# Two blocks of attention and experts on one core: gate products moved to GpSimd, the second attention reordered, zero products added

## The chip, the cores and the metric

The kernel runs on one core of one Trainium2 chip. The metric is the device time of one execution in microseconds (us); lower is better. TensorE (PE) multiplies matrices into PSUM, VectorE (DVE) and ScalarE (ACT) read and write SBUF and PSUM, GpSimd (POOL) works here on SBUF alone, SyncE issues most DMAs. Each engine runs its own instructions in program order and waits on semaphores for the others.

## The reference

`x` is (8 sequences, 128 tokens, 128 channels), float32. Four residual steps follow one another, each on a layer norm of `x`:

```python
x = x + tanh(g_xattn[0]) * xattn0(layernorm(x), ctx, ctx)   # 16 heads of 64, causal mask
x = x + tanh(g_ffn[0])   * ffn0(layernorm(x))               # 8 experts of 256 + 4 zero experts, best 2 of 12
x = x + tanh(g_xattn[1]) * xattn1(layernorm(x), ctx, ctx)   # 16 heads of 8, biases, no mask
x = x + tanh(g_ffn[1])   * ffn1(layernorm(x))               # 8 routed experts of 64, best 2 of 8, + 2 shared

# ffn1
logits = xf @ router_w + router_b
gates  = softmax(logits of the best 2, 0 elsewhere)
expert = lambda xf, w1, w3, w2: silu(xf @ w1) * (xf @ w3) @ w2
out    = sum_e gates[:, e] * expert_e(xf) + sum of the two shared experts
```

The change touches the third step (the second attention) and the fourth (the second expert step).

## The kernel before

The program is written per engine, as five lists of instructions with semaphores between them; the order on each engine is the order of the calls in its block. Three PSUM tensors of two banks (`SP`, `TP`, `OC`) are handed round by hand. The fourth, `MB`, is a ring of two banks: `ring_order()` lists every use of it in the order in which TensorE takes them, use k lies in bank k % 2, and `take(name)` makes TensorE wait until use k - 2 has been read. A new order on TensorE therefore needs a new ring order, and each use waits for the reader of the one two before it.

Second attention, sequence by sequence b = 0 to 7. `scores1(b, j)` (L1238, 32-row products, j = 0, 1 for two of the four head groups) fills an area; `max1` on DVE (L882) takes its maxima into `NM`; `maxima1(b)` on TensorE (L1258) transposes them into the ring; `shift1(b)` on DVE (L890) adds them to the queries, so that `turned1(b, j)` (L1250) gives shifted scores the other way round; `exp1(b, j)` on ACT (L571) takes their exponentials; `values_of(b)` (L1267) and `sums_of(b)` (L1274) multiply by the values and sum up; `copy_outputs(b)` on ACT (L580) and `normalise1(b)` on DVE (L895 to L906) and POOL (L414) finish them. In the loop TensorE's order for b = 3 to 6 is `values_of(b-2)`, `maxima1(b)`, `scores1(b+1, 0)`, `scores1(b+1, 1)`, `sums_of(b-2)`, `turned1(b, 0)`, `turned1(b, 1)`. DVE's is `shift1(b)`, `max1(b+1, 0)`, `max1(b+1, 1)`, `normalise1(b-2)`. The queries of sequences 4 to 7 are laid out by four products `spread_queries(i)` (L1206, L1207) and four copies `place_queries(i)` on ACT (L563); before, all four copies stand behind `exp1(1, 1)`. `output1(h, w)` (L1287) is the output projection of two sequences, `residual` on DVE (L767) adds it, statistics, `rstd_of` on POOL (L379, L380) and `normed` on DVE (L694) make the layer norm, `xn_transposes(n, h)` (L1047) turns it, `xnT_hi_copy` on ACT (L494) and `xnT_lo_copy` on DVE (L701, L702) split it in two parts; `three` (L1026 to L1028) multiplies with both.

Second expert step, ten turns n = 0 to 9 (two halves of the tokens, five pairs of experts; n = 0 and 5 are the shared pair and have no gates). `hidden1(n)` on TensorE makes the two hidden halves (six 512-column products), `silu_1(n)` on ACT (L587) takes silu of the first, `hidden1(n)` on DVE multiplies by the second (L914) and, for a routed pair, by the gates (L921), which `spread_gates(n)` (L1335) has spread over the rows in a ring bank; `expert1(n)` (L1315) is the second matrix. The gates come from `logits` (L1146), `route_best` and `route_gates` on DVE (L783 to L823) with `best_difference` on POOL (L418), `gates_turn` (L1326), `gates_hi` on ACT (L596) and `gates_lo` on DVE (L925).

`keep_clock(dst, times)` (L1033) issues products of zeros, 128 x 256 in bfloat16, whose results nobody reads: 20 at the start, 12 in `fill_wait(0)`, 10 in `gates_turn(0)`.

Of the kernel before, what the change touches and what calls it, by code (L numbers as in the profile page):

```python
# [12 lines left out]
ALU = mybir.AluOpType  # L13
# [30 lines left out]
def ring_order():  # L44
# [13 lines left out]
    uses += [("a", 2, 0), ("a", 2, 1), ("w", 0), ("t", 2, 1), ("m", 1), ("q1", 1), ("o", 0), ("m", 2)]  # L58
    uses += [("p", i) for i in range(4)]
    for b in range(3, B):  # L60
        uses += [("m", 7), ("y1", 0, 0), ("y1", 0, 1), ("o", 5)] if b == 7 else [("o", b - 2), ("m", b)]
    uses += [("o", B - 2), ("t", 3, 0), ("o", B - 1), ("l", 1, 0)]
    uses += [("y1", 1, 0), ("y1", 1, 1), ("g", 0), ("b", 1), ("t", 3, 1)]
    for n in range(2, N1):
        if pair1(n) < C1 - 1:
            uses.append(("b", n))
        uses += {2: [("l", 1, 1)], 4: [("g", 1)]}.get(n, [])
# [15 lines left out]
def build(nc, x, ctxT, mask, g_x, g_f, w0, wo0, bo0, gw0, gb0, f0w1, f0w2,  # L83
          wqk1, bqk1, wv1, bv1, wo1, bo1, gw1, gb1, f1w13, f1w2,
          ident, causal, k_rows, zeros, pairs, rev0, rev1, out):
    with ExitStack() as ctx:
# [35 lines left out]
        rstd = sb("rstd", [P, B])  # L122
        euler = sb("euler", [P, HB])
# [13 lines left out]
        S_sb = sb("S_sb", [P, 2, H4, P])  # L137
        PT = sb("PT", [P, 2, H4, P])
# [103 lines left out]
        h1_full, silu1, up1, y1_full = (sem(n) for n in ("h1_full", "silu1", "up1", "y1_full"))  # L242
        fin, stored = sem("fin"), sem("stored")
# [15 lines left out]
        def ring_read(kind, a, b=0):  # L259
# [6 lines left out]
                    "b": (up1, 2 * a + 2)}[kind]  # L266
# [102 lines left out]
        def _(pool):  # L369
# [49 lines left out]

            g.memset(warm_sb[:], 0.0).then_inc(warm_set, 1)  # L420
# [27 lines left out]
            hooks = {0: [lambda: add_bias(2, 1)], 2: [lambda: split_f1(0), lambda: split_f1(1)],  # L448
                     3: [lambda: split_f1(2), lambda: split_f1(3)], 7: [lambda: rstd_of(3, 0)]}
# [6 lines left out]
            best_difference(1, 0)  # L456
            rstd_of(3, 1)
            best_difference(1, 1)

        @block.scalar  # L460
        def _(act):
# [196 lines left out]
            hooks = {2: [lambda: split_f1(0), lambda: split_f1(1)], 3: [lambda: split_f1(2), lambda: split_f1(3)]}  # L658
# [11 lines left out]
            hooks = {1: [lambda: gates_hi(0)], 2: [lambda: xnT_hi_copy(3, 1)], 5: [lambda: gates_hi(1)]}  # L670
# [6 lines left out]
        def _(dve):  # L677
# [19 lines left out]
            def xnT_lo_copy(n, h):  # L697
                name = ("t", n, h)
                dve.wait_ge(hi_, nth(n, h))
                if n % 2:  # L700
                    v.tensor_copy(xnT[:], ring(name)).then_inc(flat_, 1)  # L701
                ins = v.tensor_tensor(xnT_lo[:, half(h)], ring(name), xnT_hi[:, half(h)].bitcast(F32), ALU.subtract)  # L702
# [205 lines left out]
            def hidden1(n):  # L908
                h, c = n // C1, pair1(n)
                dve.wait_ge(silu1, n + 1)  # L910
# [4 lines left out]
                if c == C1 - 1:  # L915
# [63 lines left out]
            max1(2, 1)  # L979
            mid = {7: [lambda: residual(1, 0, 0), lambda: residual(1, 0, 1),  # L980
                                                       lambda: stats_after(3, 0)]}
            late = {7: [lambda: normed(3, 0)]}
            for b in range(2, B):
# [6 lines left out]
                normalise1(b - 2)  # L990
# [3 lines left out]
            xnT_lo_copy(3, 0)  # L994
            normalise1(B - 1)
            route_best(1, 0)
            residual(1, 1, 0)
            residual(1, 1, 1)
# [499 lines left out]
```

## Time and profile before

| | us |
|---|---|
| median of 3 runs | 271.07 |
| lowest, highest | 268.44, 273.26 |
| the profiled execution | 270.25 |
| its span, first to last instruction | 268.5 |
| mean granted TensorE clock of the span | 0.985 |

The profiled execution lies 0.8 us under the median; 1.75 us of it lie outside the span. The three runs spread over 4.8 us, 1.8% of the median. The granted clock is a share of full speed: 1.00 is TensorE's 2.4 GHz and 0.50 its 1.2 GHz.

### The profile page before, as it was taken

What the parts mean: (1) busy time and instruction counts of PE and PEld (TensorE: products, weight loads), DVE (VectorE), ACT (ScalarE), POOL (GpSimd) and SP (SyncE); (2) the same over time, 40 slices, a digit from 0 to 9 for tenths busy, and PEclk for the clock granted to TensorE, in tenths of its full rate; (3) what the DMA queues carried; (4) which work ended last, traced back from release to release, by engine and by line L of the source; (5) the groups of instructions that cost most, each with busy time, mean ns of one, the idle gap of its engine ahead of it and who ended that gap; (6) DMA issues with size and microseconds to landing.
All of it is one profiled execution on the core that took longest, in us unless ns stands there. A gap on an engine that the chain in (4) does not pass through costs nothing.

```text
span 268.5 us, 7171 instructions
## 1 busy us (share of the span) xinstructions
PE 246.7 (92%) x2914; PEld 208.4 (78%) x2914; DVE 187.4 (70%) x487; ACT 116.2 (43%) x199; POOL 73.0 (27%) x92
## 2 busy tenths in 40 slices
PE   8879999899999999989999999998899988879993
PEld 3557778788998888768999998987577877657882
DVE  1637788967374998897256695466897994879753
ACT  2565455544441555414134445423378643421310
POOL 3355393445433633340010013000306013111000
PEclk9999999999999999999999999999799988999999
DMA  7619500040000000087680000620000000000011
GB/s 194 197 55 306 147 1 4 2 120 4 0 2 2 1 2 2 2 273 275 240 281 1 2 0 0 182 94 4 0 2 2 2 2 2 2 2 2 0 39 39
DMA packets 13233, 16.74 MB, mean 62 GB/s; under 512 B 2065, under 2 KB 10641, under 8 KB 13073
## 3 DMA queue, kind: packets, MB, share of 16 engines
q1 hardware_dynamic: 13056, 16.03, 19.0%
q8 instruction: 23, 0.38, 0.6%
q10 hardware_dynamic: 144, 0.26, 0.4%
q14 instruction: 10, 0.07, 0.1%
HBM read 12.62 MB, written 3.67 MB: 61 GB/s over the span
## 4 chain that ended last, share of the span: by engine, by line
PE 72%; DVE 14%; issue 4%; ACT 4%; POOL 2%; DMA 2%; DVEq 0%; SPq 0%
PE OC L1176 11%; PE MB L1136 5%; PE MB L1026 5%; PE SP L1097 5%; PE OC L1119 5%; PE TP L1106 5%; PE MB L1028 4%; PE MB L1027 4%; PE TP L1315 3%; PE MB L1267 2%; PE OC L1125 2%; PE SP L1026 2%; PE SP L1028 2%; PE SP L1027 2%; PE MB L1274 2%
## 5 line engine op out<-in xcount | busy, mean ns | idle before, releaser
L409 POOL TENSOR_TENSOR S_sb<-S_sb,nmax 128x512 f32<-128x512 f32 x32 | 33.2, 1041 | 38.8 <-DVE nmax L742 38.8
L839 DVE SCALAR_TENSOR_TENSOR x_sb<-OC,gate,x_sb 128x128 f32<-128x128 f32 x64 | 18.0, 345 | 22.5 <-PE OC L1176 22.5
L1176 PEld LDWEIGHTS OC<-f_w,hid 128*128 128x128 f32 x256 | 30.9, 192 | 1.4
L733 DVE TENSOR_TENSOR S_sb<-SP,maskb 128x512 f32<-128x512 f32 x32 | 21.9, 686 | 14.0 <-PE SP L1097 13.8
L1176 PE MATMUL OC<-f_w,hid 128*128 128x128 f32 x256 | 31.4, 276 | 0.0
L742 DVE TENSOR_REDUCE nmax<-S_sb 128x4 f32<-128x512 f32 x32 | 22.0, 686 | 1.1
L525 ACT ACTIVATE PT<-TP 128x512 f32<-128x512 f32 x32 | 19.0, 594 | 7.2 <-PE TP L1106 7.1
L1106 PE MATMUL TP<-id_sb,S_sb 128*128 128x128 f32 x128 | 19.5, 275 | 1.9 <-POOL S_sb L409 1.8
L1119 PE MATMUL OC<-PT,arena_f 128*32 128x128 f32 x512 | 17.7, 275 | 2.8 <-issue 2.1
L509 ACT ACTIVATE arena_f<-MB 128x512 f32<-128x512 f32 x16 | 9.6, 599 | 23.7 <-PE MB L1028 23.2
L501 ACT ACTIVATE arena_f<-MB 128x512 f32<-128x512 f32 x16 | 9.6, 599 | 23.2 <-PE MB L1028 22.4
L379 POOL TENSOR_SCALAR var_eps<-mv 128x4 f32<-128x4 f32 x8 | 2.0, 247 | 62.5 <-DVE mv L687 62.5
L1106 PEld LDWEIGHTS TP<-id_sb,S_sb 128*128 128x128 f32 x128 | 14.9, 141 | 5.0 <-POOL S_sb L409 3.4
L1097 PE MATMUL SP<-arena_f 64*128 64x128 f32 x256 | 18.6, 285 | 0.0
L1097 PEld LDWEIGHTS SP<-arena_f 64*128 64x128 f32 x256 | 15.5, 187 | 2.6 <-issue 1.8
L1119 PEld LDWEIGHTS OC<-PT,arena_f 128*32 128x32 f32 x512 | 13.3, 109 | 5.5 <-issue 4.4
L558 ACT ACTIVATE hid<-SP 128x512 f32<-128x512 f32 x16 | 9.5, 598 | 17.4 <-PE SP L1028 16.8
L558 ACT ACTIVATE hid<-TP 128x512 f32<-128x512 f32 x16 | 9.6, 599 | 14.8 <-PE TP L1028 13.8
L1136 PE MATMUL MB<-wo_sb,oT 128*128 128x128 f32 x128 | 15.0, 276 | 0.0
L1136 PEld LDWEIGHTS MB<-wo_sb,oT 128*128 128x128 f32 x128 | 14.6, 192 | 0.2 <-issue 0.2
L1315 PEld LDWEIGHTS TP<-f_w,hid 128*128 128x128 f32 x80 | 9.9, 191 | 5.5 <-DVE hid L921 3.3
L1315 PE MATMUL TP<-f_w,hid 128*128 128x128 f32 x80 | 11.1, 281 | 3.3 <-DVE hid L921 2.3
(202 smaller groups left out, 587.9 us busy)
## 6 DMA issues: line engine op xcount, KB each, us to landing
k_dram<-f_r SPq DMA_DIRECT2D x4, 512.0 KB, 8.7
arena_f<-in_zeros SPq DMA_DIRECT2D x1, 2048.0 KB, 8.6
arena_r<-k_dram SPq DMA_DIRECT2D x1, 2048.0 KB, 8.1
w_raw<-in_w SPq DMA_DIRECT2D x4, 384.0 KB, 4.0
ew_raw<-in_f0w SPq DMA_DIRECT2D x1, 1024.0 KB, 6.4
f_w<-in_f0w SPq DMA_DIRECT2D x1, 1024.0 KB, 10.3
arena_r<-q_dram SPq DMA_DIRECT2D x2, 512.0 KB, 4.1
ew_raw<-in_f1w SPq DMA_DIRECT2D x1, 640.0 KB, 9.8
```

The costliest lines, as they stand in the source:

```text
L409: g.tensor_tensor(S_sb[:, b], S_sb[:, b], nmax[:, b].unsqueeze(2).to_broadcast([P, H4, P]), ALU.add).then_inc(shifted, 1)
L525: sc.activation(PT[:, b], TP[:, b, :].rearrange("p (h q) -> p h q", h=H4), ACT.Exp).then_inc(expd, 1)
L558: sc.activation(hid[:, n % 2, c, :], bank[:, c, :], ACT.Silu).then_inc(hid_done, 1)
L733: v.tensor_tensor(S_sb[:, b].rearrange("p (r a) k -> p r a k", r=2), SP[:, :, 2 * P * b:2 * P * (b + 1)].rearrange("p r (a k) -> p r a k", ...
L742: v.tensor_reduce(nmax[:, b], S_sb[:, b], X, ALU.max, negate=True).then_inc(maxed, 1)
L1026: mm(out_, w[0], m[0], start=True, stop=False)
L1097: ins = mm(SP[:, r, P * (2 * b + p):P * (2 * b + p + 1)], qT[rows, s % 2, p, o], kT[rows, s % 2, p, o], start=True, stop=True)
L1106: ins = nc.tensor.transpose(TP[:, b, P * i:P * (i + 1)], S_sb[:, b, i, :], id_sb[:])
L1119: mm(OC[32 * hd:32 * (hd + 1), 0, P * (2 * a + b):P * (2 * a + b + 1)], v0[:, s % 2, 2 * w + b, DH0 * hd + 32 * a:DH0 * hd + 32 * (a + 1)] ...
L1136: ins = mm(bank[:, batch(b)], oT[:, k, batch(2 * w + b)], wo_sb[:, k, :], start=(k == 0), stop=(k == 7))
L1176: ins = mm(OC[:, n % 2, batch(t)], hid[:, n % 2, c, batch(t)], f0_w2[:, e, c, :], start=(c == 0), stop=(c == 1))
L1315: ins = mm(TP[:, h, batch(t)], hid[:, n % 2, 1, batch(t)], f1_w2[:, c, :], start=(first and t == 0), stop=last, skip_group_check=True)
```

## The change

What it does, stage by stage:

- The expert step: for n = 1 to 4 the gates are copied from the ring to SBUF by ACT (`gates_rows`, into the old score tile, renamed `gate_rows`), POOL multiplies silu by them (`gate_silu`), and DVE does one product instead of two. Turns 6 to 9 stay as they were. `silu_1` waits for the first hidden half alone. `output1(1, 1)`, `gates_turn(0)`, `expert1(0)`, the transposes and the logits of the second half, and the last `spread_gates` stand elsewhere in TensorE's order; residuals and statistics stand behind the first `hidden1` on DVE; `route_best(1, 0)` stands ahead of the last `normalise1`, `sums_of(7)` behind the logits.
- The flat copy of the fourth norm's transposes moves from DVE to ACT; DVE's split waits for it.
- Two one-column activations into a `spare` tile, one with Exp behind the last silu of the first expert step, one with Silu between the last outputs of the attention.
- The second attention: `spread_queries` and `place_queries` come earlier, among `turned1(1, *)` and `exp1(1, *)`; `maxima1(3)` comes ahead of `turned1(2, *)`; the splits of the expert weights (`split_f1`, ACT and POOL) come two sequences later; `normalise1(0)` comes earlier on DVE.
- Zero products: 8 ahead of `turned1(0, 0)`, 16 instead of 12 in `fill_wait`, 3, 8, 4, 4, 4, 4 ahead of the maxima of b = 2 to 7, 6 ahead of `output1(0, 1)`, 4 instead of 10 in `gates_turn(0)`. The four each at b = 4, 5 and 6 stand ahead of the fifth to the seventh maxima.

```diff
@@ ring_order
-    uses += [..., ("m", 1), ("q1", 1), ("o", 0), ("m", 2)]
-    uses += [("p", i) for i in range(4)]
+    uses += [..., ("m", 1), ("q1", 1), ("o", 0)]
+    uses += [("p", 0), ("p", 1), ("m", 2), ("p", 2), ("p", 3)]
...
+                 [("m", 3), ("o", 1)] if b == 3 else [("o", b - 2), ("m", b)])
-    uses += [("y1", 1, 0), ("y1", 1, 1), ("g", 0), ("b", 1), ("t", 3, 1)]
+    uses += [("y1", 1, 0), ("g", 0), ("y1", 1, 1), ("b", 1)]
...
+        uses += {2: [("t", 3, 1), ("l", 1, 1)], 4: [("g", 1)]}.get(n, [])
@@ gpsimd
+            def gate_silu(n):
+                pool.wait_ge(rows_full, n)
+                pool.wait_ge(silu1, n + 1)
+                g.tensor_tensor(hid[:, n % 2, 0, :], hid[:, n % 2, 0, :], gate_rows[:, n % 2, :], ALU.mult
+                                ).then_inc(gated_silu, 1)
...
             best_difference(1, 0)
+            gate_silu(1)
             rstd_of(3, 1)
+            gate_silu(2)
+            gate_silu(3)
             best_difference(1, 1)
+            gate_silu(4)
@@ scalar
+            def xnT_flat_copy(h):
+                name = ("t", 3, h)
+                wait_full(act, name)
+                act.wait_ge(logit_in, nth(1, 0) if h else nth(0, 1))
+                sc.activation(xnT[:], ring(name), ACT.Copy).then_inc(flat_, 1)
...
-                act.wait_ge(h1_full, n + 1)
+                act.wait_ge(h1_full, 2 * n + 1)
...
+            def gates_rows(n):
+                wait_full(act, ("b", n))
+                if n > 2:
+                    act.wait_ge(gated_silu, n - 2)
+                sc.activation(gate_rows[:, n % 2, :], ring(("b", n)), ACT.Copy).then_inc(rows_full, 1)
...
+            sc.activation(spare[:], tanh_g[:, 0:1], ACT.Exp)
             exp1(0, 0)
             exp1(0, 1)
             xnT_hi_copy(2, 1)
             queries1(1)
             copy_outputs(0)
+            place_queries(0)
+            place_queries(1)
             exp1(1, 0)
+            place_queries(2)
+            place_queries(3)
             exp1(1, 1)
-            for i in range(4):
-                place_queries(i)
-            hooks = {2: [... split_f1(0), split_f1(1)], 3: [... split_f1(2), split_f1(3)]}
+            hooks = {4: [... split_f1(0), split_f1(1)], 5: [... split_f1(2), split_f1(3)]}
...
             copy_outputs(B - 3)
+            sc.activation(spare[:], tanh_g[:, 0:1], ACT.Silu)
             copy_outputs(B - 2)
             xnT_hi_copy(3, 0)
+            xnT_flat_copy(0)
             copy_outputs(B - 1)
+            hooks = {1: [gates_hi(0), gates_rows(1)],
+                     2: [gates_rows(2), xnT_hi_copy(3, 1), xnT_flat_copy(1)],
+                     3: [gates_rows(3)], 4: [gates_rows(4)], 5: [gates_hi(1)]}
@@ vector
             def hidden1(n):
+                dve.wait_ge(h1_full, 2 * n + 2)
+                by_pool = 0 < n < C1
+                if by_pool:
+                    dve.wait_ge(gated_silu, n)
+                else:
+                    dve.wait_ge(silu1, n + 1)
...
-            route_best(1, 0)
-            residual(1, 1, 0)
-            residual(1, 1, 1)
-            hooks = {0: [route_gates(1, 0), stats_after(3, 1), gates_lo(0), normed(3, 1)], 1: [xnT_lo_copy(3, 1)],
-                     2: [route_best(1, 1)], ...
+            route_gates(1, 0)
+            hooks = {0: [residual(1, 1, 0), gates_lo(0), residual(1, 1, 1), stats_after(3, 1)],
+                     1: [normed(3, 1)], 2: [xnT_lo_copy(3, 1), route_best(1, 1)],
...
@@ tensor
+                if b == j == 0:
+                    keep_clock(bank[:, 0, 0:256], 8)
...
+            ZEROS = {2: 3, 3: 8, 4: 4, 5: 4, 6: 4, 7: 4}
+
             def maxima1(b):
                 name = ("m", b)
                 bank = take(name)
+                if b in ZEROS:
+                    keep_clock(bank[:, 256:512], ZEROS[b])
                 pe.wait_ge(maxed1, 2 * (b + 1))
...
-                    keep_clock(bank[:, 256:512], 10)
+                    keep_clock(bank[:, 256:512], 4)
...
             outputs1(0)
+            spread_queries(0)
+            spread_queries(1)
             turned1(1, 0)
             turned1(1, 1)
             maxima1(2)
             scores1(3, 0)
             scores1(3, 1)
-            spread_queries(0) ... spread_queries(3)
+            spread_queries(2)
+            spread_queries(3)
+            maxima1(3)
+            scores1(4, 0)
             turned1(2, 0)
             turned1(2, 1)
+            values_of(1)
+            scores1(4, 1)
+            sums_of(1)
+            turned1(3, 0)
+            turned1(3, 1)
+            for b in range(4, B):
...
                     output1(0, 0)
+                    keep_clock(area_for("t", b, 0)[:, 0, 0:256], 6)
                     output1(0, 1)
...
-            outputs1(B - 1)
+            values_of(B - 1)
             logits(1, 0)
+            sums_of(B - 1)
             hidden1(0)
+            hidden1(1)
             output1(1, 0)
+            gates_turn(0)
+            expert1(0)
             output1(1, 1)
-            hidden1(1)
-            expert1(0)
-            gates_turn(0)
-            hidden1(2)
             spread_gates(1)
-            xn_transposes(3, 1)
+            hidden1(2)
             expert1(1)
             for n in range(2, N1):
-                if pair1(n) < C1 - 1:
+                if pair1(n) < C1 - 1 and n < N1 - 1:
                     spread_gates(n)
                 if n == 2:
-                    logits(1, 1)
+                    xn_transposes(3, 1)
                 if n + 1 < N1:
                     hidden1(n + 1)
+                if n == 2:
+                    logits(1, 1)
+                if n == N1 - 2:
+                    spread_gates(N1 - 1)
                 if n == 4:
                     gates_turn(1)
                 expert1(n)
```

## Rows read from the trace of the kernel before

**Rows 1.** Windows: PE, PEld, DVE, ACT, POOL busy, granted clock, DMA share, GB/s.
```profile
185.40:188.80 3.40, 1.56 (x27) 1.26 (x27) 3.21 (x13) 2.56 (x3) 0.67 (x2) 1.00 0.02 5
188.80:192.20 3.40, 3.40 (x19) 2.45 (x18) 2.55 (x6) 0.82 (x2) 1.87 (x2) 0.51 0.00 0
192.20:219.60 27.40, 24.98 (x538) 19.99 (x537) 24.04 (x37) 18.30 (x27) 5.63 (x9) 1.00 0.01 2
219.60:222.90 3.30, 3.30 (x59) 2.92 (x61) 1.74 (x9) 1.94 (x2) 1.12 (x2) 0.50 0.02 5
222.90:264.00 41.10, 35.78 (x348) 29.79 (x338) 30.41 (x92) 10.68 (x18) 4.37 (x7) 1.00 0.03 8
```

**Rows 2.** Timeline, start of the second attention: start us, us, instructions, idle before them.
```profile
186.23 1.28 ACT L571 ACT_TABLE_LOAD   x1 [4.58 <-PE MB L1250]
...
187.52 1.02 ACT L571 ACTIVATE oT<-MB 128x1024 f32<-128x1024 f32 x1
...
188.60 2.55 PE L1033 MATMUL MB<-warm_sb 128*128 128x256 bf16 x12 [1.24 <-ACT oT L571]
189.44 1.14 DVE L694 SCALAR_TENSOR_TENSOR xn<-x_sb,mv,rstd 128x128 f32<-128x128 f32 x4 [0.36 <-POOL rstd L380]
```

**Rows 3.** Timeline, the zero products of gates_turn(0).
```profile
236.04 1.26 PE L1033 MATMUL MB<-warm_sb 128*128 128x256 bf16 x10
```

**Rows 4.** Timeline: the first place_queries, and the maxima of b = 4, 5 and 7.
```profile
198.90 1.08 ACT L563 ACTIVATE arena_r<-MB 128x512 fp32r<-128x512 f32 x2
...
206.52 0.33 PE L1258 MATMUL MB<-id_sb,NM 128*128 128x128 f32 x1
...
210.37 0.33 PE L1258 MATMUL MB<-id_sb,NM 128*128 128x128 f32 x1
...
217.68 0.30 PE L1258 MATMUL MB<-id_sb,NM 128*128 128x128 f32 x1 [0.56 <-DVE NM L882]
```

**Rows 5.** Timeline, end of the second attention and start of the routing.
```profile
220.76 1.94 PE L1267 MATMUL MB<-arena_f 128*32 128x128 f32 x32
...
225.13 1.30 DVE L694 SCALAR_TENSOR_TENSOR xn<-x_sb,mv,rstd 128x128 f32<-128x128 f32 x4
...
227.13 1.08 PE L1267 MATMUL MB<-oT,arena_f 128*32 128x128 f32 x32
...
229.22 1.06 PE L1146 MATMUL MB<-gw_sb,xnT 128*128 128x8 f32 x8
...
229.57 0.31 DVE L895 STREAM_TRANSPOSE sumT<-o_sb 128x128 f32<-128x128 f32 x1 [0.41 <-ACT o_sb L580]
...
230.76 0.18 DVE L794 TENSOR_TENSOR logit<-MB,gb_sb 128x32 f32<-128x32 f32 x1
...
233.53 0.88 DVE L767 SCALAR_TENSOR_TENSOR x_sb<-MB,tanh_g,x_sb 128x256 f32<-128x256 f32 x2
```

**Rows 6.** Timeline, route_gates' first and last, expert1 of n = 0, 1, 4, 9.
```profile
234.91 0.17 DVE L808 TENSOR_SCALAR rs<-rs 128x4 f32<-128x4 f32 x1
235.05 0.97 PEld L1315 LDWEIGHTS TP<-f_w,hid 128*128 128x128 f32 x8 [1.44 <-DVE hid L914]
...
235.85 0.22 DVE L823 TENSOR_TENSOR gate<-rt 128x64 f32<-128x64 f32 x1
...
241.82 1.16 PE L1315 MATMUL TP<-f_w,hid 128*128 128x128 f32 x8 [0.79 <-DVE hid L921]
...
251.66 1.06 PE L1315 MATMUL TP<-f_w,hid 128*128 128x128 f32 x8
...
264.00 1.16 PE L1315 MATMUL TP<-f_w,hid 128*128 128x128 f32 x8 [1.07 <-DVE hid L921]
```

**Rows 7.** Groups of instructions by form: busy, mean ns of one, idle before.
```profile
L409 POOL TENSOR_TENSOR S_sb<-S_sb,nmax 128x512 f32<-128x512 f32 x32 | 33.2, 1041 | 38.8 <-DVE nmax L742 38.8
...
L392 POOL TENSOR_TENSOR f_lo<-ew_raw,f_hi 128x512 fp32r<-128x512 f32 x4 | 5.1, 1272 | 7.4 <-ACT f_hi L476 7.4
...
L921 DVE TENSOR_TENSOR hid<-hid,MB 128x512 f32<-128x512 f32 x8 | 5.5, 688 | 0.8
```

More of the change, by code:

```diff
@@ L122, in build @@
         rstd = sb("rstd", [P, B])
+        spare = sb("spare", [P, 1])
         euler = sb("euler", [P, HB])
@@ L265, in ring_read @@
                     "p": (placed, a + 1), "a": ((maxed1, 1), (maxed1, 2), (expd1, 1))[a if kind == "a" else 0],
-                    "b": (up1, 2 * a + 2)}[kind]
+                    "b": (rows_full, a) if a < C1 else (up1, 2 * a + 2)}[kind]
         def area_read(kind, b, j):
@@ L447, in _ @@
             rstd_of(2, 1)
-            hooks = {0: [lambda: add_bias(2, 1)], 2: [lambda: split_f1(0), lambda: split_f1(1)],
-                     3: [lambda: split_f1(2), lambda: split_f1(3)], 7: [lambda: rstd_of(3, 0)]}
+            hooks = {0: [lambda: add_bias(2, 1)], 4: [lambda: split_f1(0), lambda: split_f1(1)],
+                     5: [lambda: split_f1(2), lambda: split_f1(3)], 7: [lambda: rstd_of(3, 0)]}
             for b in range(B):
@@ L699, in xnT_lo_copy @@
                 dve.wait_ge(hi_, nth(n, h))
-                if n % 2:
+                if n == 1:
                     v.tensor_copy(xnT[:], ring(name)).then_inc(flat_, 1)
+                elif n == 3:
+                    dve.wait_ge(flat_, nth(1, h))
                 ins = v.tensor_tensor(xnT_lo[:, half(h)], ring(name), xnT_hi[:, half(h)].bitcast(F32), ALU.subtract)
@@ L979, in _ @@
             max1(2, 1)
+            normalise1(0)
             mid = {7: [lambda: residual(1, 0, 0), lambda: residual(1, 0, 1),
@@ L989, in _ @@
                     hook()
-                normalise1(b - 2)
+                if b > 2:
+                    normalise1(b - 2)
                 for hook in late.get(b, ()):
@@ L994, in _ @@
             xnT_lo_copy(3, 0)
+            route_best(1, 0)
             normalise1(B - 1)
-            route_best(1, 0)
-            residual(1, 1, 0)
-            residual(1, 1, 1)
-            hooks = {0: [lambda: route_gates(1, 0), lambda: stats_after(3, 1), lambda: gates_lo(0), lambda: normed(3, 1)], 1: [lambda: xnT_lo_copy(3, 1)],
-                     2: [lambda: route_best(1, 1)], 3: [lambda: route_gates(1, 1)], 4: [lambda: gates_lo(1)],
+            route_gates(1, 0)
+            hooks = {0: [lambda: residual(1, 1, 0), lambda: gates_lo(0), lambda: residual(1, 1, 1), lambda: stats_after(3, 1)],
+                     1: [lambda: normed(3, 1)], 2: [lambda: xnT_lo_copy(3, 1), lambda: route_best(1, 1)],
+                     3: [lambda: route_gates(1, 1)], 4: [lambda: gates_lo(1)],
                      5: [lambda: finish(0, 0), lambda: finish(0, 1)]}
@@ L1037, in fill_wait @@
                 name = ("w", b)
-                done(name, keep_clock(take(name)[:, 0:256], 12))
+                done(name, keep_clock(take(name)[:, 0:256], 16))
             def xn_transposes(n, h):
@@ L1303, in hidden1 @@
                     o = slice(2 * P * c + P * k, 2 * P * c + P * (k + 1))
-                    ins = three((OC, SP)[n % 2][:, k, :], (f1_hi[:, o], f1_lo[:, o]), (xnT_hi[:, half(h)], xnT_lo[:, half(h)]))
-                ins.then_inc(h1_full, 1)
+                    three((OC, SP)[n % 2][:, k, :], (f1_hi[:, o], f1_lo[:, o]), (xnT_hi[:, half(h)], xnT_lo[:, half(h)])
+                          ).then_inc(h1_full, 1)
             def expert1(n):
@@ L1403, in _ @@
             scores1(3, 1)
-            spread_queries(0)
-            spread_queries(1)
+            spread_queries(2)
+            spread_queries(3)
+            maxima1(3)
+            scores1(4, 0)
             turned1(2, 0)
-            spread_queries(2)
             turned1(2, 1)
-            spread_queries(3)
-            for b in range(3, B):
+            values_of(1)
[4 more added lines that the diff above has]
+            for b in range(4, B):
                 if b == B - 1:
```

18 lines of the change are left out of this document (10 added, 8 removed).

## Prediction

> **What bounds the kernel now.** I read the granted clock by windows first, then the timeline of the last 80 us, then the groups by form. Up to 185 us nothing changes, so the question is the last third. There the clock is at half speed twice, for about 3.4 us each [rows 1]. Ahead of the first dip PE was busy 1.56 of 3.40 us [rows 1]: it waits for the exponentials of sequence 0, which wait for an activation table load of 1.28 us [rows 2]. The second dip falls where the last maxima and the output projection alternate with DVE. Between the dips the clock is full for 27.4 us with PE busy 24.98 and DVE 24.04 [rows 1]: the attention loop holds both engines at once. A turn of it takes 210.37 - 206.52 = 3.85 us [rows 4]. In the expert step the clock is full throughout [rows 1]; its first turns follow a chain through DVE (PE waits for L921 at n = 1), the last ones are PE-bound [rows 6].
>
> I followed the new orders by hand, with durations from these rows, and give the result at milestones, as shift against before.
>
> **First maxima to the fifth, +1.0.** The Exp load goes to where ACT idled before (4.58 us, [rows 2]), so 1.28 us leave the path. But the 8 zero products ahead of `turned1(0, 0)` stand on it: one costs 1.26/10, some 0.11 us started back to back at full clock [rows 3], so 0.86 us, and score products that ran beside each other are parted, 0.4 more. The first exponential starts where it did. `fill_wait` gets 16 products: 1.7 us at full clock against 2.55 for 12 at half [rows 2]. If the clock holds, the transposes start as soon as `normed` is done at 190.58, 0.7 us earlier in the end. That gain is spent at once. `spread_queries` 0 and 1 now stand ahead of `turned1(1, *)`, and their two copies (0.54 each, [rows 4]) ahead of `exp1(1, 0)`; the next two stand ahead of `exp1(1, 1)`, which moves from 197.9 to about 200.9 and holds `turned1(2, *)`. I find the third maxima at +0.4, the fourth earlier (they no longer wait for `turned1(2, *)`), and the fifth at 207.5 against 206.52, four zero products among it: +1.0. A table load hidden that costs nothing needs ACT idle; it is.
>
> The Trainium skill (ScalarE: Activation LUTs, What ACT_TABLE_LOAD costs) adds a drain of about 1.38 us to each load; here the exponential starts at 187.52, right behind the load that began at 186.23 [rows 2], so 1.28 is taken off and not 2.66. By the page this stage would come out 1.4 us better, and the whole at 270.6.
>
> **Fifth to seventh maxima, +0.9.** The loop's ring goes: maxima, shift on DVE, `max1(b+1, 0)` on DVE, `turned1(b, 1)`, `values_of`, next maxima. Four zero products between `values_of` and the maxima lengthen it by 0.43, since PE does not wait for DVE there: the maxima come 3.3 us after the last ones' start, PE is there at 3.85. Two more sets, at b = 5 and 6: 0.86. The clock was full there already [rows 1], so nothing is bought. The set at b = 7 falls into the 0.56 us in which PE waits for L882 [rows 4], the 6 at `output1(0, 1)` into a wait of about the same length: nothing. If that cover were gone they would cost 0.43 and 0.64.
>
> **To `normed(3, 0)`, -1.4.** If the second dip goes, 32 products of `values_of` cost 1.08 us and not 1.94 [rows 5], and with the turned scores and the sums some 1.5 us leave the path through `copy_outputs(5)` and `normalise1(5)`, on which `normed` at 225.13 [rows 5] waited in DVE's order. So `normed(3, 0)` starts at about 225.6: +0.4 in all. The Silu load stands between two copies with 1.4 us between them; it moves nothing.
>
> **To `expert1(0)`, +1.0.** ACT now makes the flat copy (0.6 us) ahead of DVE's split, in place of DVE's own 0.69: even. `sums_of(7)` waits behind the logits, whose bank needs that split (ring use k - 2), so it moves from 228.0 to about 230.4, and `hidden1(0)` from 230.1 to 231.4. DVE does `route_best` first (230.76 to 233.5, 2.8 us [rows 5]), which covers this; then `normalise1(7)`, 229.57 to 230.76 before, 1.2 us [rows 5]; then `route_gates`, 234.91 to 236.07 [rows 6]. From logits that end at 230.4: 230.5 + 2.85 + 1.2 + 1.2 = 235.75, gates 0.3 us earlier. POOL's power of 1 us hides behind `normalise1(7)`. But the first product of `hidden1(0)` now stands behind the gates on DVE: 235.75 + 0.7, so `expert1(0)` starts at 236.45 against 235.05 [rows 6]: +1.4 in all.
>
> **To `expert1(1)`, -2.1.** Behind it DVE does one residual (0.45), `gates_lo`, the other residual and statistics; PE spreads the gates at about 237.95. ACT copy 0.6, POOL product, one DVE product 0.69 [rows 7]. POOL's product is not in the trace: two full 128 x 512 inputs, so I take L392's 1.27, the nearest; L409's 1.04, with one input a repeated column, is the low end; with DVE working beside it I allow 1.5 as the high end (an estimate, 1.27 and a fifth). `expert1(1)` starts at 238.4 + 0.65 + 1.35 + 0.75 = 241.15 against 241.82 [rows 6]: -0.7 in all. The `normed(3, 1)` that stood ahead of it on DVE comes behind, and POOL's `rstd_of(3, 1)` waits for the first `gate_silu`.
>
> **To `expert1(4)`, +3.2.** Here the change is a longer chain: `spread_gates(n)` is issued behind `expert1(n-1)`, and then spread, ACT copy, POOL product, DVE product follow in series: 0.95 (expert products) + 0.25 + 0.2 + 0.65 + 1.3 + 0.75 = 4.15 with handovers. Before, the ring bank was read by DVE directly, and expert 1 to 4 took 251.66 - 241.82 = 9.84 us [rows 6], 3.3 a turn. After: 241.15, 245.8 (waits for the late `normed(3, 1)` and the logits too), 249.95, 254.15. ACT and PE have time to spare there; `hidden1(n+1)` of 1.4 us fits in the chain. So DVE loses one product of 0.69 a turn and gains nothing: +2.5 in all.
>
> **To the end, -0.7.** Turns 6 to 8 are PE-bound before and after (2.54 us each). The last `expert1` waited for silu and two products [rows 6]; silu now starts at the first half, 0.6 earlier, and the last spread costs PE nothing on that chain: 265.8 against 264.00, +1.8.
>
> The sum: +1.0 + 0.9 - 1.4 + 1.0 - 2.1 + 3.2 - 0.7 = +1.8 (with rounding). Against the profiled execution's own 270.25 that gives 272.0, span 270.3. The median shown is 0.8 above the profiled time; I leave it out, because what sets runs apart may be dips of this kind, and the change removes two. Bounds: POOL at 1.04 or 1.5 moves four links by 0.23 each: -0.9, +0.9; hand-overs in the followed orders, 1 us either way.
>
> The Trainium skill (GPSIMD Engine Reference, Performance versus the Vector engine) measures a two-input float32 product of 2048 columns at 4497 ns; a quarter is 1.12 us, an estimate. By it the sum would be 0.6 lower. Its Engine selection section gives elementwise products to VectorE, which speaks against this move; the chain above agrees.
>
> **Rivals.**
> (a) *The gates chain is no loss.* If DVE's own order (`route_best`, `route_gates`, normalisations) really set turns 2 to 4, the freed products pay: DVE is busy 30.41 of the last 41.10 us [rows 1]. Then those turns stay at 3.3 and 2.5 of the 3.2 fall away; with POOL at 1.04 another 0.9: 268.6. If further low-clock stretches that this one execution does not show are usual before (273.26 is 3 us above it), a median after could lie another 2 to 4 lower: 265 to 266. Against it: the hand-over count above.
> (b) *The zeros do not hold the clock.* They don't do what they are for: in one or both old places it still falls. Each costs what it cost: 0.7 and 1.5, and 16 zero products at half clock take 3.4 us and not 1.7, 0.9 more. 272.0 + 2 to 3 = 274.5.
> (c) *New waits bring new dips.* PE now waits 0.9 us for `normed(3, 0)` and 1.1 us more for the split at 228.4 to 229.5 with little work between, about as much idle time as ahead of the first dip (1.84 of 3.4 us, [rows 1]); and 1.4 us a turn for the gates at n = 1, 3 and 4. A dip at half clock over 3.4 us of PE-bound work costs up to 1.7 us; over the chained turns about 1. It is slower by over 2% only if four or five fall, or with POOL at 1.5: two dips and 0.9 give 276, three 277.5. For it: such waits did bring dips. Against it: the waits at n = 0 and 1 before were about 1 us and the clock stayed full [rows 1].
>
> **Chances.** Forecast as summed, dips gone, 0.45. (a) 0.25, of it 0.1 under 2%. (b) 0.12. (c) 0.18, half of it beyond 2%. 2% is 5.4 us, about what a measurement of this kernel, whose three runs spread over 4.8 us, tells from no change. Faster 0.12, within 2% 0.78, slower 0.10. The range: from (a)'s upper part, 267.0, to (c) with two dips, 276.0.
>
> **What would show it.** Right: clock 1.00 from 186 to 225; maxima 4.28 us apart at b = 4 to 6; ACT's Exp load at about 181.7; `normed(3, 0)` near 225.6; expert1 of n = 1 to 4 over 4 us apart, each waiting for the DVE product behind POOL; POOL products near 1.27 us. Wrong: turns of 3.3 us, a half-clock window between 225 and 255, or maxima still 3.85 apart.

## The result and the profile after

| | before | after |
|---|---|---|
| median of 4 runs each | 272.16 us | 280.06 us |
| lowest, highest | 268.44, 273.47 | 279.14, 280.99 |
| after / before, 95% interval | | 1.038 (1.027 to 1.049) |
| profiled execution | 270.25 | 279.14 |
| its span and mean granted clock | 268.5, 0.985 | 277.4, 0.973 |

The change makes the kernel 3.8% slower. The ratios leave out executions in the slower of two states: here 280.06 stands against before's 268.44 and 271.07, for e1 to e4 before is three executions at 268.0, and for the later kernels it is executions of 268.0 to 272.0, so kernels of different groups are compared by their spans. The four spans after are 277.2 to 279.2 at clocks of 0.963 to 0.973. Before ran 70 times more beside the runs below. One of these took 1310.75 us at full clock and is left out; the other 69 have a mean span of 270.4 and clocks of 0.959 to 1.000. In the eight with the clock at 0.999 or more the span is 266.2 to 266.6; I take 266.4. I call such a span, with next to no time at half clock, a clean one.

Windows of the kernel after (columns as in [rows 1]):

```profile
188.80:192.20 3.40, 2.55 (x20) 1.90 (x20) 3.04 (x6) 1.67 (x3) 2.06 (x3) 1.00 0.00 0
...
197.30:200.70 3.40, 3.04 (x41) 2.24 (x38) 2.62 (x6) 2.14 (x4) 0.46 (x1) 1.00 0.03 5
200.70:214.30 13.60, 13.28 (x166) 10.17 (x168) 5.21 (x8) 6.65 (x10) 1.43 (x3) 0.50 0.00 1
214.30:272.90 58.60, 50.78 (x678) 41.99 (x674) 41.58 (x115) 23.77 (x38) 14.41 (x18) 1.00 0.02 6
```

Both half-clock stretches of [rows 1] are gone, as forecast. A third, longer one has come: 200.7 to 214.3. In it PE is busy 13.28 of 13.60 us, DVE only 5.21: the attention waits for TensorE at 1.2 GHz. The timeline shows what TensorE did as it fell:

```profile
198.54 0.66 PE L1282 MATMUL TP<-arena_r 32*128 32x128 f32 x8
...
199.16 0.66 PE L1282 MATMUL OC<-arena_r 32*128 32x128 f32 x8
...
199.66 0.44 PE L1250 MATMUL MB<-q_hi,ctxT_lo 32*128 32x512 f32 x2
...
199.94 0.39 PE L1251 MATMUL MB<-q_lo,ctxT_lo 32*128 32x512 f32 x2
200.37 1.08 ACT L583 ACTIVATE arena_r<-MB 128x512 fp32r<-128x512 f32 x2 [1.26 <-PE MB L1251]
...
201.03 1.89 PE L1077 MATMUL MB<-warm_sb 128*128 128x256 bf16 x8 [0.69 <-ACT arena_r L583]
```

They are score products and `spread_queries`, each on 32 rows of the array, and then TensorE waits 0.69 us for `place_queries`. The eight zero products of the fourth maxima come at 201.03, after the fall, and take 1.89 us where [rows 3] has ten in 1.26; the clock stayed low behind them.

The milestones by which the prediction went, as start us:

| | before | after | shift | forecast |
|---|---|---|---|---|
| first exponential | 187.52 | 188.38 | +0.9 | 0 |
| fourth maxima, b = 3 | 201.98 | 202.71 | +0.7 | earlier |
| fifth maxima, b = 4 | 206.52 | 213.56 | +7.0 | +1.0 |
| seventh maxima, b = 6 | 214.21 | 222.39 | +8.2 | +1.9 |
| `normed(3, 0)` | 225.13 | 231.69 | +6.6 | +0.4 |
| `expert1(0)` | 235.05 | 242.62 | +7.6 | +1.4 |
| `expert1(1)` | 241.82 | 247.48 | +5.7 | -0.7 |
| `expert1(4)` | 251.66 | 261.17 | +9.5 | +2.5 |
| `expert1(9)` | 264.00 | 272.89 | +8.9 | +1.8 |

Of the 0.9 at the first exponential, 0.7 were there at the first maxima already (183.30 against 182.63). So nearly the whole miss lies between the first maxima and the fifth, and 6.3 us of it between the fourth and the fifth.

### The profile page after: what moved, and what is told of

Same layout as the page of the kernel before. It is cut to its first block, busy times and chain, and to the rows that moved or that the text cites. A ratio compares the mean times of both kernels' runs of the same rounds, so it can differ in the third digit from the quotient of the medians.

```text
span 277.4 us, 7260 instructions
## 1 busy us (share of the span) xinstructions
PE 255.4 (92%) x2953; PEld 214.0 (77%) x2953; DVE 185.1 (67%) x481; ACT 119.8 (43%) x207; POOL 78.2 (28%) x96
## 4 chain that ended last, share of the span: by engine, by line
PE 75%; DVE 9%; issue 4%; POOL 4%; ACT 4%; DMA 2%; POOLq 0%; DVEq 0%; SPq 0%; ACTq 0%
PE OC L1220 10%; PE MB L1180 5%; PE MB L1070 5%; PE SP L1141 5%; PE OC L1163 5%; PE TP L1150 4%; PE MB L1071 4%; PE MB L1072 4%; PE MB L1077 3%; PE TP L1365 3%; PE MB L1317 2%; PE MB L1324 2%; PE SP L1070 2%; PE OC L1169 2%; DMA w_raw<-in_w 2%
## 6 DMA issues: line engine op xcount, KB each, us to landing
f_w<-in_f0w SPq DMA_DIRECT2D x1, 1024.0 KB, 10.2
```

## The experiments

Three stages are taken apart: the zero products, the order around `spread_queries` (below, the spread order), and the expert step. The first four start from the kernel after; the `f` kernels build the change up from a version without these three; `g` and `h` follow up. In the code cuts some lines are shortened, several calls stand on one line, and lines that follow from those shown are left out. Clocks and spans are those of single executions. A mean clock does not say where the half clock fell: before's 17 executions at 0.967 span 271.5 to 274.2. So a comparison at a like clock is rough.

**e1_no_loop_zeros.** Leaves out the four zeros each at b = 4, 5, 6.

```diff
-            ZEROS = {2: 3, 3: 8, 4: 4, 5: 4, 6: 4, 7: 4}
+            ZEROS = {2: 3, 3: 8, 7: 4}
```

> The changed kernel without the four zero products each at b = 4, 5 and 6. Theory 1 (the loss is the 13.5 us at half clock that begin at 200.7 us, ahead of these products): the dip stays, and these products cost 0.43 us each at full clock and 0.9 at half (one set): 278 to 279. Theory 2 (they help the clock back up after the dip): without them the dip lasts longer, 281 or more. Theory 3 (they are themselves the loss): below 276.

Median 277.56 (276.59 to 278.50), 1.035 (1.029 to 1.042) of before, between the ranges of theories 1 and 3. At a clock of 0.973 the span is 276.1 and 275.4, against 277.4 after: 1.3 and 2.0 for three sets, of which the one at b = 4 lies in the half-clock stretch. Timeline of the kernel after, the zeros and the maxima of b = 5, then those of b = 6:

```profile
217.71 0.61 PE L1077 MATMUL MB<-warm_sb 128*128 128x256 bf16 x4
...
218.15 0.27 PE L1308 MATMUL MB<-id_sb,NM 128*128 128x128 f32 x1
...
222.39 0.27 PE L1308 MATMUL MB<-id_sb,NM 128*128 128x128 f32 x1
```

The same maxima of e1:

```profile
217.25 0.33 PE L1308 MATMUL MB<-id_sb,NM 128*128 128x128 f32 x1
...
221.10 0.33 PE L1308 MATMUL MB<-id_sb,NM 128*128 128x128 f32 x1
```

A turn takes 4.24 with four zeros and 3.85 without, which is that of before [rows 4]: 0.39 a set at full clock, where 0.43 was summed. The long half-clock stretch is there in e1 too, so these zeros neither cause nor cure it.

**e2_old_spread.** The order of `spread_queries`, `place_queries` and the fourth maxima as before, in the ring, on ACT and on PE.

```diff
-    uses += [("p", 0), ("p", 1), ("m", 2), ("p", 2), ("p", 3)]
+    uses += [..., ("m", 2)]
+    uses += [("p", i) for i in range(4)]
-                 [("m", 3), ("o", 1)] if b == 3 else [("o", b - 2), ("m", b)])
+        uses += (... if b == 7 else [("o", b - 2), ("m", b)])
...
-            place_queries(0), place_queries(1), exp1(1, 0), place_queries(2), place_queries(3), exp1(1, 1)
+            exp1(1, 0), exp1(1, 1), place_queries(0) ... place_queries(3)
...
-            spread_queries(0) ... spread_queries(3), maxima1(3), turned1(2, 0), turned1(2, 1)
+            spread_queries(0), spread_queries(1), turned1(2, 0), spread_queries(2), turned1(2, 1), spread_queries(3)
+            for b in range(3, B):
```

> The changed kernel with spread_queries, place_queries and the fourth maxima back in the order of before; all zero products stay. Theory 1 (the new order with its thin work and its wait for the copies lets the clock fall at 200.7): the dip is gone, 5 to 6 us back, 273 to 275. Rival (the new expert step makes the loss): no change within 1 us, 279 to 281.

Median 275.15 (274.22 to 275.39), 1.025 (1.020 to 1.031). Clocks 0.981 to 0.991, spans 272.4 to 273.3: the long stretch is gone and 5 us with it. In its profile a short one, 3.4 us, stands in the expert step, between 250.5 and 254.5.

**e3_old_experts.** The expert step as before, everything else as after: gates multiplied on DVE, old order on all engines.

```diff
-                by_pool = 0 < n < C1
+                by_pool = False
...
```

> The changed kernel with the whole expert step of before (gates on DVE, its order on every engine). Theory 1: the dip at 200.7 stays, and only the chain through POOL goes, worth the +1.8 that stood at the end of my sum against +0.4 at the start of the fourth norm, plus 0.9 for one DVE instruction held while POOL worked: 277 to 279. Rival (the expert step makes the loss): 272 to 273.

Median 276.10 (273.23 to 279.07), 1.026 (1.010 to 1.043); spans 271.4 to 277.2 at clocks 0.985 to 0.960. The half-clock stretch is still there (200.9 to 211.2 in its profile). So it is a matter of the attention.

**e4_zeros_at_spread.** Eight zeros more, between the two pairs of `spread_queries`.

```diff
+                if i == 2:
+                    keep_clock(bank[:, 0:256], 8)
```

> The changed kernel with 8 more zero products, into the ring bank of the third spread_queries ahead of it, 0.86 us at full clock on the path. Theory 1 (too little work in the stretch before 200.7): the dip goes, 5 to 6 us back less 0.9: 274 to 276. Rival (zero products do not hold the clock there, or the dip has another cause): 280 to 281.

Median 279.35 (274.31 to 283.06): two executions with clocks of 0.999 and 0.988 and spans of 272.5 and 273.9, two with 0.957 and spans of 281.1 and 281.2. It holds half the time. The execution at 0.999 is the only one that shows the whole change at a full clock: 272.5 less 0.86 for these eight zeros makes 271.6 for the kernel after, an estimate from one execution, against 266.4 before. So 5.2 of the slowdown is work and order.

The profiled execution, the one at 0.988, keeps the clock in the attention; two short half-clock stretches, 3.4 us each, stand in its expert step, between 244.0 and 248.0 and between 254.5 and 258.5. So it shows the new spread order at full clock:

```profile
197.30:200.70 3.40, 3.40 (x41) 2.69 (x40) 2.68 (x4) 1.47 (x2) 0.45 (x1) 1.00 0.02 5
200.70:214.30 13.60, 12.87 (x295) 10.31 (x295) 9.18 (x15) 10.02 (x15) 3.19 (x5) 1.00 0.01 2
...
208.81 0.27 PE L1310 MATMUL MB<-id_sb,NM 128*128 128x128 f32 x1
```

The last line is its fifth maxima, 4.75 us ahead of those of the kernel after, with eight zeros more.

**f0_base.** From the kernel after, without the loop zeros, with the old spread order and the old expert step. What is left of the change are the early table loads, `split_f1` later, `normalise1(0)` earlier, and the other zeros.

```diff
-            ZEROS = {2: 3, 3: 8, 4: 4, 5: 4, 6: 4, 7: 4}
+            ZEROS = {2: 3, 3: 8, 7: 4}
...    (and the edits of e2 and of e3)
```

> The changed kernel with the old expert step, the old order of spread_queries, place_queries and the fourth maxima, and without the zero products at b = 4, 5 and 6: what stays are the early table loads, the later weight splits, the earlier normalise1(0) and the zero products at b = 0, 2, 3, 7 and in fill_wait. Theory (these zeros hold the clock in the two old places, and nothing else of the change is needed for that): clock 0.995 or more in every execution, 266 to 268. Rival (the clock falls all the same): 270 to 273 with executions far apart.

Median 270.11 of 10 runs (268.24 to 273.11), 0.997 (0.992 to 1.002). Mean clock 0.992, mean span 268.4; clean spans 266.4 to 266.9, up to 0.5 above before's 266.4. This part of the change costs next to nothing and steadies the clock: three of ten executions at 0.999 or more, eight of 69 before. Against what I had expected, it does not hold it in every execution: in its profile the clock is still at half for 3.4 us between 188.5 and 192.5, the first of the two old places.

**f1_base_new_experts, f2_base_new_spread, f3_base_pool_gates.** One part added to f0 each: the whole new expert step; the new spread order; or only POOL's product, with the copy on ACT, in the old order of the expert step.

```diff
+                by_pool = 0 < n < C1                          # f1, f3
+    uses += [("y1", 1, 0), ("g", 0), ("y1", 1, 1), ("b", 1)]  # f1, and its orders
+    uses += [("p", 0), ("p", 1), ("m", 2), ("p", 2), ("p", 3)] # f2, and its orders
```

> f0_base with the new expert step alone put back. At a like clock 2.5 to 3.5 us above f0_base: 2.5 from the followed chain, 0.9 for the DVE instruction held beside POOL. Rival (the new expert step is even by itself): within 1 us of f0_base.

> f0_base with the new order of spread_queries, place_queries and the fourth maxima alone put back. Theory: a half-clock stretch of 10 us or more from about 200 us in at least half of the executions, worth 4 to 6 us: median 271 to 274, and at full clock within 1 us of f0_base. Rival (the order is harmless without the loop's zeros and the new experts): 266 to 268 in all executions.

> f0_base with the four gate products moved to POOL (ACT copy, POOL product, one DVE product) and every order otherwise as before. The chain of spread, copy, POOL, DVE takes the place of the DVE pair: each of turns 1 to 4 takes 4.2 us or more where it took 3.3: 3 to 5 us above f0_base. Rival (DVE's own order bounds these turns, so less work on it pays): at or below f0_base.

- f1: median 272.51 of 10 (271.56 to 274.31), 1.009 (1.004 to 1.015). At clocks of 0.991 to 0.993 the span is 270.3 to 270.7, against 268.1 to 269.1 of f0 at 0.992 to 0.994: +2.0 in the mean, a little under what I had expected.
- f2: median 278.76 (277.82 to 281.30), 1.031 (1.019 to 1.044); clocks 0.943 to 0.960, spans 276.0 to 279.5. The median is 5 us over the top of what I had expected, and all four executions show it. The spread order alone gives nearly as long a span as the whole change.
- f3: median 277.03 (276.55 to 278.50), 1.024 (1.011 to 1.038). At clocks of 0.985 and 0.986 its spans are 275.2 and 274.7, where f0 has 269.4 at 0.984: some 5.5 slower, where f1 is 2.0. The new orders win back more than half of what POOL's product costs. In f3's profile 10.2 us at half clock lie in the expert step itself (between 239.5 and 250.0), so the two parts are not cleanly apart.

Windows of f2:

```profile
197.30:199.80 2.50, 2.50 (x32) 1.79 (x29) 1.78 (x3) 1.36 (x2) 0.46 (x1) 1.00 0.03 7
199.80:223.50 23.70, 23.01 (x329) 17.97 (x331) 13.15 (x20) 10.84 (x17) 4.32 (x7) 0.50 0.01 1
```

The clock falls although PE is busy all 2.50 us ahead of it, and stays low for 23.7 us of a PE that is busy 23.01. Idle time right ahead of the fall, as my rivals had it, isn't what f2 shows.

The old order is no guard against the fall itself. Windows of f1, which has it:

```profile
197.60:201.00 3.40, 3.40 (x40) 2.75 (x40) 3.19 (x5) 3.04 (x5) 0.46 (x1) 1.00 0.02 5
201.00:204.40 3.40, 3.40 (x41) 2.47 (x41) 0.00 (x0) 2.43 (x3) 0.00 (x0) 0.50 0.00 0
```

There too the clock falls at the end of the 32-row products, with PE busy throughout, but it is back after 3.4 us. By windows of 0.5 us this is so in three of the eight profiled executions with the old order (f1, g3, h1); the other five have no fall there. All six with the new order and no zeros added at this place (after, e1, e3, f2, g1, g4) fall and stay low for 10.2 to 23.7 us. What the new order brings is the length.

**g1_exp_before_copies.** f2 with `exp1(1, 1)` ahead of the last two `place_queries` on ACT. It tests whether the fall comes from the copies that hold up the exponentials (A); else TensorE's order (B) is left.

```diff
-            place_queries(2), place_queries(3), exp1(1, 1)
+            exp1(1, 1), place_queries(2), place_queries(3)
```

> f2_base_new_spread (277.1 us mean span, clock 0.943 to 0.960) with one step moved on ACT: exp1(1, 1) ahead of the third and fourth place_queries, so that turned1(2, *) and values_of(1) need not wait for them. Theory A (the held exponential starves PE of its dense products, and that lets the clock fall): clock 0.98 or more and 270 to 272. Theory B (the thin order on PE up to 200.7 us, which this leaves as it is, lets it fall): still 275 to 279.

Spans 274.7, 276.2 and 277.3 at clocks of 0.954 to 0.966, and once 267.5 at 0.999; median 277.87. The clock still falls in three of four: against A, and for B only as what is left. TensorE's wait of 0.69 us for the third copy is still there in g1, so this run does not part the thin products from that wait; h2 does.

**g2_base_no_zeros.** f0 without any of the added zeros, `fill_wait` at 12.

```diff
-            ZEROS = {2: 3, 3: 8, 7: 4}
+            ZEROS = {}
-                done(name, keep_clock(take(name)[:, 0:256], 16))
+                done(name, keep_clock(take(name)[:, 0:256], 12))
```

> f0_base (median 270.1, clock 0.978 to 1.000) without any of the added zero products: 12 in fill_wait as before, none at b = 0, 2, 3, 7. If the added zeros hold the clock: it spends more time at half speed, 0.967 to 0.985, and 271 to 273. If they do not matter: 269 to 270 with the same clock; at full clock it should be up to 0.9 faster than f0_base.

Median 271.58 of 10 (269.49 to 283.12), 1.003 (0.997 to 1.009). Mean clock 0.977, mean span 271.0, against 0.992 and 268.4 of f0. None of the ten executions reaches 0.999. The zeros outside the loop raise the clock. What they are worth in time is less sure: 2.6 in the mean, but 1.8 of it are two executions of 274.8 and 281.3; the other eight have a mean of 269.2.

**g3_new_order_gates_on_dve.** f1 with the gates multiplied on DVE as before, in the new orders.

```diff
-                by_pool = 0 < n < C1
+                by_pool = False
-            gate_silu(1) ... gate_silu(4), gates_rows(1) ... gates_rows(4)
```

> f1_base_new_experts (median 272.5) with the gates multiplied on DVE as before, but all orders of the new expert step kept. If the loss of the expert step is the chain through POOL: 3 us faster, 268.5 to 270, at or below f0_base. If it is the new orders: within 1 us of f1_base_new_experts.

Median 271.03 of 10 (269.50 to 273.60), 1.001 (0.996 to 1.006). At clocks of 0.991 to 0.993 the span is 267.7 to 268.0, against 270.3 to 270.7 of f1: the way over ACT and POOL costs 2.5. Timeline of f1, `expert1` of n = 2, 3 and 4:

```profile
246.63 1.14 PE L1362 MATMUL TP<-f_w,hid 128*128 128x128 f32 x8
...
251.50 1.46 PE L1362 MATMUL TP<-f_w,hid 128*128 128x128 f32 x8 [2.10 <-DVE hid L953]
...
256.31 1.16 PE L1362 MATMUL TP<-f_w,hid 128*128 128x128 f32 x8
```

The same of g3:

```profile
245.59 1.14 PE L1357 MATMUL TP<-f_w,hid 128*128 128x128 f32 x8
...
250.10 1.16 PE L1357 MATMUL TP<-f_w,hid 128*128 128x128 f32 x8 [1.74 <-DVE hid L955]
...
253.17 1.06 PE L1357 MATMUL TP<-f_w,hid 128*128 128x128 f32 x8
```

From n = 2 to n = 4 f1 takes 9.7 us and g3 7.6. The turn into n = 3 is over 4.5 us long in both; it is the turn into n = 4 that POOL makes longer, 4.81 against 3.07. Some 0.5 of this is half clock, which f1's profile has from 252.0 to 255.4: in the kernel after, at full clock, the same turn takes 261.17 - 256.84 = 4.33.

**g4_dense_zeros_in_dip.** f2 with 24 zeros ahead of the fifth maxima, inside the low stretch.

```diff
-            ZEROS = {2: 3, 3: 8, 7: 4}
+            ZEROS = {2: 3, 3: 8, 4: 24, 7: 4}
```

> f2_base_new_spread with 24 zero products ahead of the fifth maxima, inside the half-clock stretch: 2.6 us at full clock, 5.1 at half. Theory (at half clock the loop's own products are too thin to bring the clock back, dense ones do): the stretch ends at them, near 214 us, instead of lasting to 224; clock 0.965 or more, and the time 275 to 278 in spite of the added work. Rival (they do nothing to the clock): 280 to 283.

Median 277.33 (276.62 to 279.01), 1.030 (1.020 to 1.040). The time is as the theory had it, but not for its reason. In its profile the clock is back at about 211.9, and the 24 zeros start at 211.97 and take 2.79 us, at full clock: it came back just ahead of them. Whether dense work can end such a stretch is not shown.

**h1_base_early_silu.** f0 with silu waiting for the first half alone and the last `spread_gates` a turn earlier.

```diff
-                act.wait_ge(h1_full, 2 * n + 2)
+                act.wait_ge(h1_full, 2 * n + 1)
+                if n == N1 - 2:
+                    spread_gates(N1 - 1)
```

> f0_base with silu_1 waiting for the first hidden half alone and the last spread_gates one turn earlier, as in the changed kernel; gates stay on DVE. My step for the end said -0.7: at a like clock 0.5 to 0.7 below f0_base (266.4 to 266.9 of span at full clock), so a span of 265.8 to 266.3 at full clock and a median of 269 to 270. Rival (the end is bound by PE or DVE and not by silu): no difference at a like clock.

Median 269.79 of 12 (267.65 to 272.55), 0.995 (0.990 to 1.001). Clean spans 265.8 to 266.3, against f0's 266.4 to 266.9: some 0.6 gained. It is the fastest kernel of the study, though its interval just reaches no change.

**h2_spread_with_dense_zeros.** f2 with sixteen zeros more at the place where the clock falls: eight ahead of the third maxima, eight ahead of the third `spread_queries`.

```diff
-            ZEROS = {2: 3, 3: 8, 7: 4}
+            ZEROS = {2: 11, 3: 8, 7: 4}
+                if i == 2:
+                    keep_clock(bank[:, 0:256], 8)
```

> f2_base_new_spread (clock 0.943 to 0.960, mean span 277.1) with 8 more zero products ahead of the third maxima and 8 ahead of the third spread_queries, 1.7 us of work at full clock, in the stretch before the clock falls. If thin work lets it fall: clock 0.985 or more in nearly all executions, mean span 269 to 271. If it falls for another reason: clock below 0.97 and 277 to 280.

Median 270.86 of 12 (270.56 to 273.45), 1.003 (0.998 to 1.007), against 278.76 of f2. Mean clock 0.998. Windows of h2:

```profile
197.30:200.70 3.40, 3.40 (x49) 2.70 (x46) 1.82 (x3) 1.45 (x2) 0.45 (x1) 1.00 0.02 5
200.70:214.30 13.60, 12.88 (x304) 10.30 (x303) 10.56 (x16) 10.02 (x15) 3.33 (x5) 1.00 0.01 2
```

In the same 13.6 us TensorE runs 304 products where the kernel after ran 166, and DVE is busy 10.56 and not 5.21. Sixteen products that nobody reads, 1.7 us of work, take 7.8 us off the mean span (277.1 to 269.3).

h2 also keeps TensorE's wait for the third `place_queries`, ahead of the zeros of the fourth maxima:

```profile
202.07 1.05 PE L1069 MATMUL MB<-warm_sb 128*128 128x256 bf16 x8 [0.68 <-ACT arena_r L579]
```

The kernel after waits 0.69 us there. So this wait alone does not bring the low clock.

## Why the prediction failed

**Where the time went.** Mean span 278.1 after, 270.4 before: 7.7. By the clean spans 5.2 of it is work and order (271.6, an estimate, against 266.4). The rest is what half clock cost in each, 6.5 after against 4.0 before. Of the 5.2, measured by parts at like clock: 2.0 the expert step (f1 against f0), 1.2 the three sets of loop zeros (0.39 each, e1), 0.6 to 0.8 the spread order (h2's 269.0 at full clock, less 1.7 for its zeros, is 267.3, and g1's one clean span is 267.5, against f0's mean of 266.7). Some 1.3 is not assigned.

**The step that failed: "First maxima to the fifth, +1.0", with "If the clock holds".** The milestone came 7.0 late, and 0.7 of it was there before the stage. The order that I followed was right as far as it went. The profiled execution of e4 keeps the clock through this stretch, and its fifth maxima stand at 208.81, 2.3 behind before's. Of this, 0.3 was there at the first maxima (182.96 against 182.63) and 0.86 are its own eight zeros; the 1.1 left, an estimate, is the +1.0 of the sum. The other 5.3 of the 7.0 are the half clock from 200.7 to 214.3, which the sum put at nothing, because I looked for falls of the clock only where PE would stand idle.

What the runs show in its place: the new spread order makes TensorE stay at half clock for 10.2 to 23.7 us (f2 against f0, e2 against the kernel after), and sixteen dense products in it bring the clock back to 1.00 (h2). What in the order does so is argued and not shown. Products of 32 rows behind one another are not enough. Before, nothing but these and one transposition ran on TensorE from 196.26 to 200.97, and the clock was full:

```profile
197.30:200.70 3.40, 3.40 (x41) 2.58 (x41) 3.13 (x4) 3.07 (x5) 0.00 (x0) 1.00 0.03 5
```

Nor is the wait for `place_queries` enough, by h2. The two together are not tested apart from the zeros. Why the clock then stays low with a busy TensorE is open, and so is why it falls in some executions of e4 and g1 and not in others.

Rival (c) had new dips, but at the routing and in the expert step, and priced one at 1.7 us at most. None came there in the profiled execution of the kernel after, and the one that came earlier lasted 13.6 us. That size is why the measured time lies outside the range. In other profiles short ones did come where (c) looked, between 231 and 258 us: of 3.4 us each in e2, e4, f1 and g3, and one of 10.2 us in f3. But f2 and g1, with the old expert step, have 6.8 us there too, so the new waits are not shown to be their cause. Of the signs named for "wrong" none appeared; of those for "right" the clock of 1.00 from 186 to 225 and `normed(3, 0)` near 225.6 failed.

**"Fifth to seventh maxima, +0.9": right.** It was +1.1: 0.39 a set, by e1's turns, and the last 0.7 us of the half-clock stretch. "Nothing is bought" holds in full.

**"To `normed(3, 0)`, -1.4": right.** The dip at 219.6 went; from the fifth maxima on the shift fell by 0.4, where +0.9 and -1.4 make -0.5. The Silu load moved nothing:

```profile
230.41 0.39 ACT L600 ACTIVATE o_sb<-MB 128x256 f32<-128x256 f32 x1
230.81 1.28 ACT L698 ACT_TABLE_LOAD   x1
...
232.11 0.20 ACT L698 ACTIVATE spare<-tanh_g 128x1 f32<-128x1 f32 x1
232.22 0.37 ACT L600 ACTIVATE o_sb<-MB 128x256 f32<-128x256 f32 x1
```

The activation starts 0.02 us after the load ends, so 1.28 is the whole cost of a load here, as I took it.

**The first exponential "starts where it did": right.** 188.38 against 187.52, of it 0.7 from before this stage; the hidden load and the eight zeros cancel. That the clock holds there was right for the kernel after, but not for every execution: in the profiles of f0 and g1, with the same zeros, it falls there for 3.4 us.

**"To `expert1(0)`, +1.0" and "To `expert1(1)`, -2.1": right.** +1.0 and -1.9.

**"To `expert1(4)`, +3.2": right mechanism, 0.6 too small.** It was +3.85. The turns took 4.50, 4.86 and 4.33. Rival (a), that DVE's freed product would pay, falls with g3: the same orders with the gates on DVE are 2.5 faster. What the sum lacked is in the timeline of the kernel after, turn n = 3:

```profile
253.39 0.60 ACT L614 ACTIVATE S_sb<-MB 128x512 f32<-128x512 f32 x1 [1.91 <-PE MB L1385]
...
254.07 1.33 POOL L427 TENSOR_TENSOR hid<-hid,S_sb 128x512 f32<-128x512 f32 x1 [3.19 <-ACT S_sb L614]
254.07 0.19 DVE L821 TENSOR_TENSOR rt<-rt,rs 128x32 f32<-128x32 f32 x1
...
254.29 1.15 DVE L822 TENSOR_TENSOR rt<-rt,rev_sb 128x32 f32<-128x32 f32 x1
...
255.48 0.19 DVE L823 TENSOR_REDUCE rs<-rt 128x4 f32<-128x32 f32 x1
...
256.10 0.69 DVE L956 TENSOR_TENSOR hid<-hid,SP 128x512 f32<-128x512 f32 x1
...
256.84 1.16 PE L1365 MATMUL TP<-f_w,hid 128*128 128x128 f32 x8 [2.08 <-DVE hid L956]
```

The four links stand here in series: copy 0.60, POOL 1.33, DVE 0.69, `expert1`. POOL's product, the one cost that was bounded and not known, took 1.28 to 1.33 against the 1.27 taken. By the estimate of 1.12 from the Trainium skill (GPSIMD Engine Reference, Performance versus the Vector engine), whose figure is for an addition and not for a product, the chain would have come out too short. But L822, a product of 32 columns that took 0.19 at 252.95, takes 1.15 and ends just behind POOL's (255.44, 255.40). It is `route_best`, queued ahead of `hidden1(3)` on DVE, and it carries 0.7 us into the turn: POOL is done at 255.40, DVE's product starts at 256.10. The Trainium skill (GPSIMD Engine Reference, Key points) says that GpSimd shares its SBUF interfaces with VectorE and contends with its instructions with two SBUF inputs; the trace agrees, and gives the size: 0.96 us, the rest of POOL's product. All five profiled kernels with POOL's product in the new orders show it at this place, with 1.15 us (after, e1, e2, f1) and 1.21 us (e4).

**"To the end, -0.7": right.** -0.6; and h1, which has this step alone, gains 0.6.

**The sums.** The terms of the chain add up to 4.10 and not 4.15, and the seven shifts to +1.9, given as +1.8. A zero product is 1.26/10 = 0.13 by the row; the 0.11 taken was nearer to what it cost in the loop, 0.39/4 = 0.10. In (c) three dips at 1.7 each alone give 277.1, over 2% above before's 271.07, so "only if four or five fall" does not follow at that price.

**The base of the sum.** I added +1.8 to a profiled execution that held two dips and counted their end as the change's gain. Clean against clean, the same sum says 270.3 against 266.4, +3.9, and the estimate from e4 is +5.2. So even with a full clock this change is slower by about 2%, and f0 shows that most of the clock's gain was to be had without it.

## What to carry to other kernels

Before a new order of thin products is costed at full clock, ask what the clock does under it: here such an order cost 8.7 us in the mean span (f2 against f0) and under 1 us at full clock, and a busy PE in the records was no sign that the clock would hold. A hand-followed order can be right to 0.1 us and the forecast still wrong. Put zero products where the clock falls and nowhere else: the same four products bought nothing in the loop, where DVE and PE already ran full, and sixteen bought 7.8 us at the right place. A product moved to POOL pays only if its engine's queue was the bound; here it lengthened a chain, and one small two-input instruction of DVE beside it was held until it ended.

## What the runs showed that I had not expected

- The clock fell with TensorE busy 2.50 of 2.50 us in the records (f2), and came back only after 13.6 us (after) and 23.7 us (f2) in which it was busy over 97%.
- One instruction of VectorE with two SBUF inputs, 0.19 us by itself, took 1.15 us beside a GpSimd product. The one before it (L821), started at the same 254.07 as GpSimd's, took its usual 0.19.
- The same place can fall for 3.4 us under one order (f1, g3, h1) and for 10.2 us or more under another.
- Four spans of one kernel (e4) fall into two pairs, 272.5 and 273.9, 281.1 and 281.2: a single order can lie at the edge of holding its clock, and a few runs then tell little.
